# Scattered token rows that carry both routing weights: one row buffer with a weight on each side, sent without rewriting the weight in between

## The chip, the cores and the metric

The kernel runs on one core of a Trainium2 chip. The metric is the device time of one execution in microseconds (us), the median of the runs shown. The engines are named as the profile names them: PE (TensorE matmul; PEld is its weight load), DVE (VectorE), ACT (ScalarE), POOL (GpSimd), SP (SyncE, which here only issues DMAs).

## The reference, cut to what matters

Two layers work on `x` (4 batches of 1024 rows of 256 floats) and a context of 4 x 64 rows. The first layer shifts and compresses a memory, adds it to `x`, normalizes, and then runs a mixture of experts: each of the 4096 rows goes to its top 2 of 8 experts, and the two results are added with weights that are the square roots of a softplus.

```python
logits = jnp.einsum('btd,ed->bte', X, routing_W) + expert_bias
activation = jnp.sqrt(jax.nn.softplus(logits))
top_vals, top_idx = jax.lax.top_k(activation, K)          # K = 2
combine = jnp.sum(jax.nn.one_hot(top_idx, E) * top_vals[..., None], axis=-2)
...
hdn = jax.nn.silu(jnp.einsum('nd,edh->enh', Xf, rW1) + rb1[:, None, :])   # h = 128
y = jnp.einsum('enh,ehd->end', hdn, rW2) + rb2[:, None, :]
routed = jnp.einsum('ne,end->nd', cf, y).reshape(B, T, d)
return shared + routed
```

The second layer is a cross attention with 16 heads and another mixture of 8 experts with hidden width 384. The change touches only the routed experts of the first layer.

## The kernel before, in words

Every engine has its own program, written out by hand in the order in which it runs; semaphores tie them together. A tile is 128 rows, and there are 32 tiles. The first layer's experts are worked in two groups `g` of 16 tiles (`LT = 16`).

**Choosing.** `choose(g)` on DVE finds the two experts of each row and, through `places`, the place of each row in a table in DRAM, `xs_dram` (`XS`). A slot is 128 places of that table, all of one expert; each group has 40 slots (`LS = 40`), so 80 in all. `choose(g)` ends by writing the first weight into column `D` of the row buffer `N0` (line 1679) and the second into `m2` (line 1680), and signals `rout` (line 1682).

**Sending.** A row of `N0` is 260 floats: 256 data, the weight, three zeros. `send_rows(g)` on POOL waits for `rout` and writes each tile of `N0` to `xs_dram` by an indirect DMA, one for the first expert of its rows (`k = 0`) and one for the second (`k = 1`): 32 sends a group, 64 in all, on line 541. Between the two the weight in the row has to be replaced. So POOL sends 16 tiles with the first weight, then for each half of the group waits until those sends have landed (line 554), copies the second weights into the rows (line 555), drains, and sends the eight tiles again:

```python
for t, done in parts:
    po.wait_ge(s[done], 16 * half * (g + 1))
    po.tensor_copy(N0[:, t:t + half, D:D + 1], m2[:, t:t + half].rearrange("p (t a) -> p t a", a=1))
    po.drain()
    send(1, t, t + half, "l_sc2")
```

POOL runs `send_rows(0)`, `send_rows(1)` and then collects group 0's results (line 566).

**The slots.** SP, in `routed_rows(g)`, waits for all of the group's sends, loads slot `j` into one of eight buffers `fx` (line 397; six slots ahead) and stores the result `fy` (line 405). PE transposes the slot (`xpose`, line 857), multiplies by the first weight matrix (`up`), and by the second (`down`). For each slot PE and DVE read the slot's expert number into a register (`value_load`; TENSOR_LOAD in the lists below). DVE copies the expert's weights to `fw1` (line 1700) and the transposed rows to `fxT` (line 1702). ACT does the silu (line 1236) and scales the result by the weight that came with the rows (line 1242). PE runs `routed(0)`, then `shared(1)` (the shared expert of the second half), then `routed(1)`, and after a meeting of all engines comes the second layer. `shared_add` on DVE (line 1688) is put between slots. In the second layer rows go to `xs_dram` too, by line 616, with both weights in the row; its experts' results are scattered by line 628.

Of the kernel before, what the change touches and what calls it, by code (L numbers as in the profile page):

```python
# [36 lines left out]
P = 128  # L37
NB, T, D = 4, 1024, 256
DC = D // P
S = 64  # L40
# [48 lines left out]
def build(nc, x, ctx_in, conv_w, conv_b, rout_w, rout_b, sw1, sb1, sw2, sb2, rw1, rb1, rw2, rb2,  # L89
          wq, bq, wk, bk, wv, bv, wo, bo, wr, w1, w2, w3, out):  # L90
    st = ExitStack()
    with st:
        st.enter_context(nc.allow_non_contiguous_dma(reason="bias columns and router weights, small"))

        def sb(name, shape, dt=F32, stack=st):
            return stack.enter_context(nc.sbuf_tensor(name, shape, dt))
# [57 lines left out]
        wcol = sb("wcol", [P, 4])  # L154
# [17 lines left out]
        N0 = sb("N0", [P, TILES, XW], stack=s1)  # L172
# [26 lines left out]
        fx = [sb(f"fx{k}", [P, XW], stack=s2)[:, :] for k in range(XB)]  # L199
# [29 lines left out]
        def row_tile(m):  # L229
# [46 lines left out]
            l_sa l_sb l_sc2 l_nr l_tp l_xa l_xd l_lg l_lt l_tn l_ev l_su l_hs l_sy l_xu  # L276
            f_tp f_xt f_h f_hs f_y f_ys
            l_ga l_gb
            n_st n_q n_r n_ra wr_p wr_c t_p xt_a ro_p ro_sb
# [40 lines left out]
        def _(sp):  # L320
# [7 lines left out]
            def memory_rows(b):  # L328

                t0, k = b * BT, S // RATE  # L330
                sp.dma_start(N0[:, t0:t0 + 4, 0:D],
                             x[b, k:k + CONV, :].rearrange("(t p) d -> p t d", p=P)).then_inc(s[f"s_in{b}"], 16)
                sp.dma_start(N0[:, t0 + 4:t0 + 7, 0:D],
                             x[b, CONV + S:T - S, :].rearrange("(t p) d -> p t d", p=P)).then_inc(s[f"s_in{b}"], 16)
                sp.dma_start(N0[0:S, t0 + 7, 0:D], x[b, T - S:T, :]).then_inc(s[f"s_in{b}"], 16)
                sp.dma_start(N0[S:P, t0 + 7, 0:D], ctx_in[b]).then_inc(s[f"s_in{b}"], 16)

# [44 lines left out]
            def routed_rows(g):  # L382

                for done in ("l_sa", "l_sb"):
                    sp.wait_ge(s[done], 8 * LT * (g + 1))
                sp.wait_ge(s["l_sc2"], 16 * LT * (g + 1))
# [57 lines left out]
            for sent in ("l_sa", "l_sb"):  # L444
                sp.wait_ge(s[sent], 8 * LT * LG + 16 * FREED)
# [27 lines left out]
        def _(po):  # L473
# [38 lines left out]
            po.memset(N0[:, :, D:XW], 0.0)  # L512
# [25 lines left out]
            def send(k, t0, t1, done):  # L538

                for t in range(t0, t1):  # L540
                    po.indirect_dma_start(  # L541
                        XS, bass.IndirectOffsetOnAxis(ap=slot[k][:, t:t + 1], axis=0),
                        N0[:, t, :], None).then_inc(s[done], 16)

            def send_rows(g):
# [3 lines left out]
                half = LT // 2  # L549
                parts = [(LT * g, "l_sa"), (LT * g + half, "l_sb")]  # L550
                for t, done in parts:
                    send(0, t, t + half, done)
                for t, done in parts:
                    po.wait_ge(s[done], 16 * half * (g + 1))
                    po.tensor_copy(N0[:, t:t + half, D:D + 1], m2[:, t:t + half].rearrange("p (t a) -> p t a", a=1))
                    po.drain()
                    send(1, t, t + half, "l_sc2")
# [1647 lines left out]
```

## Time and profile before

| what | value |
|---|---|
| time, median of 3 runs | 926.6 us (926.23, 926.6, 931.65) |
| the profiled execution: its own time | 930.99 us |
| its span in the profile | 929.2 us |
| granted TensorE clock, mean share of full | 0.933 |
| busy PE / DVE / ACT / POOL | 85% / 55% / 53% / 46% |
| sends of line 541 | 64, together 64.3 us busy |
| PE's share of the chain that ended last | 54% |

The span is what the profile's rows add up to; the execution's own time is 1.8 us longer. The profiled execution was 4.4 us slower than the median of the timed runs. A share of the span is a mean over stages with different limits, so the rows further down are read by stage.

### The profile page before, as it was taken

The numbers are of one execution on the slowest core, as the hardware profiler recorded it, in microseconds if no ns is written. First come the engines' busy times: TensorE is split into PE (matmuls) and PEld (weight loads), VectorE is DVE, ScalarE is ACT, GpSimd is POOL, SyncE is SP. The second block draws the span as 40 slices with busy tenths as digits, with TensorE's granted clock in tenths as the row PEclk, the third lists the DMA queues.
The fourth block names the chain that finished last, engine by engine and source line by source line (L and its number), as shares of the span: only waits on it lengthen the run. The fifth ranks groups of instructions, "written<-read, shape, count | busy, mean of one in ns | idle before, by whom it ended". The sixth has DMA issues, their size and how long they took to land.

```text
span 929.2 us, 16520 instructions
## 1 busy us (share of the span) xinstructions
PE 792.1 (85%) x4538; PEld 684.7 (74%) x4538; DVE 509.5 (55%) x1345; ACT 490.0 (53%) x1374; POOL 429.3 (46%) x398
## 2 busy tenths in 40 slices
PE   2989883579999679999998999785789999999992
PEld 1636542479688568999987888674689999999991
DVE  5847851245265558889888878672122222244242
ACT  1458641146466468888776686341334444444440
POOL 2201657610577258988645678435552222222221
PEclk9899995589999889999998999898789999999996
DMA  8799974456699694384230244613332222256524
GB/s 260 267 298 341 318 254 144 127 163 203 156 201 242 173 333 79 62 203 84 59 115 1 80 149 137 199 47 103 97 98 75 69 67 66 70 180 200 187 89 158
DMA packets 122115, 143.02 MB, mean 154 GB/s; under 512 B 10391, under 2 KB 113612, under 8 KB 121004
## 3 DMA queue, kind: packets, MB, share of 16 engines
q1 hardware_dynamic: 90520, 92.03, 33.2%
q0 software_dynamic: 19856, 38.88, 15.4%
q10 hardware_dynamic: 11654, 11.05, 3.7%
q8 instruction: 44, 0.72, 0.3%
q14 instruction: 41, 0.34, 0.1%
HBM read 71.28 MB, written 70.65 MB: 153 GB/s over the span
## 4 chain that ended last, share of the span: by engine, by line
PE 54%; DVE 15%; ACT 9%; issue 7%; another core or an unknown queue 6%; DVEq 5%; DMA 2%; SPq 1%; POOL 1%; POOLq 0%; ACTq 0%
PE psum L678 29%; PE psum L1042 5%; ACT pr L1324 5%; PE psum L1047 5%; PE psum L1043 5%; DVE nmx L2013 2%; PE psum L1056 2%; DVE sm L2018 2%; PE psum L857 2%; PE psum L954 2%; DVE prl L2028 2%; PE psum L1026 2%; DVEq L2019 1%; DVE wlo L1983 1%
## 5 line engine op out<-in xcount | busy, mean ns | idle before, releaser
L628 POOL DMA_INDIRECT yk_dram<-ys,L x71 | 70.0, 986 | 202.2 <-ACT ys L1396 200.3
L566 POOL DMA_INDIRECT X<-yl_dram,slots_y x64 | 104.1, 1627 | 73.2 <-DMA yl_dram<-fy 50.8
L1042 PE MATMUL psum<-whi,xTh 128*128 x284 | 111.0, 391 | 22.8 <-ACT xTh L1378 22.7
L1324 ACT ACTIVATE pr<-psum,nmx 128x64 f32<-128x64 f32 x512 | 108.1, 362 | 35.2 <-DVE nmx L2013 35.2
L2107 DVE TENSOR_TENSOR hs<-psum,hs 128x384 f32<-128x384 f32 x71 | 39.7, 560 | 153.6 <-PE psum L1047 100.0
L678 PE MATMUL psum<-w_sb,cz 128*128 x426 | 104.7, 382 | 1.5 <-ACT ys L1396 1.2
L541 POOL DMA_INDIRECT xs_dram<-N,slots x64 | 64.3, 1005 | 87.3 <-DVEq L1681 50.6
L1043 PE MATMUL psum<-wlo,xTh 128*128 x284 | 97.8, 344 | 0.0
L608 POOL TENSOR_TENSOR pr<-pr,sm 128x1024 f32<-128x1024 f32 x32 | 63.8, 1992 | 57.5 <-DVE sm L2020 56.9
L678 PEld LDWEIGHTS psum<-w_sb,cz 128*128 128x128 f32 x426 | 75.8, 191 | 10.1 <-issue 2.6
L1047 PE MATMUL psum<-whi,xTl 128*128 x284 | 75.4, 347 | 3.4 <-DVE xTl L2126 3.4
L616 POOL DMA_INDIRECT xs_dram<-N,slots x64 | 66.6, 1040 | 21.3 <-issue 18.0
L1042 PEld LDWEIGHTS psum<-whi,xTh 128*128 128x128 f32 x284 | 55.0, 194 | 27.6 <-issue 26.1
L678 PE MATMUL psum<-rw_sb,fh 128*128 x160 | 57.2, 441 | 19.3 <-issue 10.6
L1384 ACT ACTIVATE cz<-psum 128x384 f32<-128x384 f32 x69 | 33.8, 490 | 71.7 <-PE psum L1056 52.8
L1390 ACT ACTIVATE hs<-psum 128x384 f32<-128x384 f32 x71 | 34.9, 492 | 60.4 <-PE psum L1047 43.5
L678 PE MATMUL psum<-fxT,fw 128*128 128x128 f32 x320 | 53.3, 292 | 9.1 <-issue 8.6
L1236 ACT ACTIVATE fh<-psum,fw 128x128 f32<-128x128 f32 x80 | 29.3, 366 | 52.2 <-remote 32.2
L1396 ACT ACTIVATE ys<-psum,wcol 128x256 f32<-128x256 f32 x71 | 33.6, 474 | 43.6 <-PE psum L678 40.4
L1043 PEld LDWEIGHTS psum<-wlo,xTh 128*128 128x128 f32 x284 | 55.3, 195 | 1.6
L1047 PEld LDWEIGHTS psum<-whi,xTl 128*128 128x128 f32 x284 | 52.8, 194 | 4.4 <-DVE xTl L2126 4.3
L1700 DVE COPY fw<-rw_sb 128x257 f32 x80 | 25.7, 321 | 54.5 <-ACT fh L1236 35.6
(338 smaller groups left out, 1917.1 us busy)
## 6 DMA issues: line engine op xcount, KB each, us to landing
fx<-xs_dram SPq DMA_DIRECT2D x80, 130.0 KB
xs_dram<-fill SPq DMA_DIRECT2D x4, 2600.0 KB
yl_dram<-fy SPq DMA_DIRECT2D x80, 128.0 KB
xs<-xs_dram SPq DMA_DIRECT2D x71, 130.0 KB
wlo<-in_L_ffn_W_dram SPq DMA_DIRECT2D x4, 1536.0 KB, 7.2
ym<-yk_dram ACTq DMA_DIRECT2D x12, 512.0 KB
xs_dram<-cz SPq DMA_DIRECT2D x1, 5200.0 KB, 27.5
xs_dram<-cz SPq DMA_DIRECT2D x8, 650.0 KB
```

What stands on the lines that cost most here:

```text
L541: po.indirect_dma_start(XS, bass.IndirectOffsetOnAxis(ap=slot[k][:, t:t + 1], axis=0), N0[:, t, :], None).then_inc(s[done], 16)
L566: po.indirect_dma_start(X[:, t, :], None, YL[b // 2], bass.IndirectOffsetOnAxis(ap=slot_y[k][:, t:t + 1], axis=0), compute_op=ALU.add).the ...
L608: po.tensor_tensor(v, v, sm[n % 2][:, :].rearrange("p (a b) -> p a b", b=1).to_broadcast([P, NHEAD, S]), ALU.mult).then_inc(s["a_pn"], 1)
L616: po.indirect_dma_start(XS1, bass.IndirectOffsetOnAxis(ap=slot[k][:, t:t + 1], axis=0), row_tile(t)[:, part], None).then_inc(s[done], 16)
L628: po.indirect_dma_start(YK, bass.IndirectOffsetOnAxis(ap=yid[:, j:j + 1], axis=0), ys[j % YB], None).then_inc(s[f"y_out{j % YB}"], 16)
L678: return nc.tensor.matmul(o, l, r, start=start, stop=stop)
L1042: nc.tensor.matmul(o, xTh[b][:, c, :], wh[c], start=c == 0, stop=False)
L1043: nc.tensor.matmul(o, xTh[b][:, c, :], wl[c], start=False, stop=False)
L1047: last = nc.tensor.matmul(o, xTl[b][:, c, :], wh[c], start=False, stop=c == DC - 1)
L1324: last = act(pr[b][:, S * h:S * h + S], bank[2 * b + h // 8][:, S * (h % 8):S * (h % 8) + S], ACT.Exp, bias=nmx[:, h:h + 1])
L1390: act(hs[j % 2], bank[2 + j % 2][:, 0:H1], ACT.Silu).then_inc(s["e_hs"], 1)
L2107: tt(hs[j % 2], bank[4 + j % 2][:, 0:H1], hs[j % 2], ALU.mult).then_inc(s["e_hg"], 1)
```

## The change

The row buffer gets a weight on each side: two columns, the data, two columns (`X0 = 2`). `choose` writes the first weight into column `X0 - 1`, left of the data, and the second into column `X0 + D`, right of it. The send for the first expert takes columns 0 to 257 (left weight and data), the one for the second takes columns 2 to 259 (data and right weight); each writes 258 floats at an element address, so that the data always fall on columns 2 to 257 of the place in `xs_dram`. The table was zeroed, so one of a place's two weight columns holds the weight and the other zero. Neither rewriting nor waiting is left between the sends. The weight of a place is the sum of both columns: the eight `fx` buffers become one tile `fx8`, and DVE adds both columns for four slots at once into `wcol`, after its copies for slot `j` with `j % 4 == 1`, once the loads of the next two slots have landed. ACT scales by `wcol`, and in every fourth slot first waits for DVE's copy of two slots later.

```diff
-        wcol = sb("wcol", [P, 4])
+        wcol = sb("wcol", [P, XB])
...
-        N0 = sb("N0", [P, TILES, XW], stack=s1)
+        N0w = sb("N0", [P, TILES, XW], stack=s1)
+        N0 = N0w[:, :, X0:X0 + D]
...
-        fx = [sb(f"fx{k}", [P, XW], stack=s2)[:, :] for k in range(XB)]
+        fx8 = sb("fx8", [P, XB, XW], stack=s2)
+        fx = [fx8[:, k, :] for k in range(XB)]
...
-                for done in ("l_sa", "l_sb"):
-                    sp.wait_ge(s[done], 8 * LT * (g + 1))
-                sp.wait_ge(s["l_sc2"], 16 * LT * (g + 1))
+                for k in range(2):
+                    sp.wait_ge(s[f"l_s{k}{g}"], 16 * LT)
...
             def send(k, t0, t1, done):
 
+                part = (slice(0, X0 + D), slice(X0, XW))[k]
                 for t in range(t0, t1):
                     po.indirect_dma_start(
-                        XS, bass.IndirectOffsetOnAxis(ap=slot[k][:, t:t + 1], axis=0),
-                        N0[:, t, :], None).then_inc(s[done], 16)
+                        XS1, bass.IndirectOffsetOnAxis(ap=slot[k][:, t:t + 1], axis=0),
+                        N0w[:, t, part], None).then_inc(s[done], 16)
...
                 po.wait_ge(s["rout"], g + 1)
-                half = LT // 2
-                parts = [(LT * g, "l_sa"), (LT * g + half, "l_sb")]
-                for t, done in parts:
-                    send(0, t, t + half, done)
-                for t, done in parts:
-                    po.wait_ge(s[done], 16 * half * (g + 1))
-                    po.tensor_copy(N0[:, t:t + half, D:D + 1], m2[:, t:t + half].rearrange("p (t a) -> p t a", a=1))
-                    po.drain()
-                    send(1, t, t + half, "l_sc2")
+                for k in range(2):
+                    send(k, LT * g, LT * g + LT, f"l_s{k}{g}")
...
-                    act(fy[j % YB], bank[(7, 5)[j % 2]][:, 0:D], ACT.Copy, scale=fx[j % XB][:, D:D + 1]).then_inc(s["f_ys"], 1)
+                    if j % 4 == 0:
+                        ac.wait_ge(s["f_xt"], j + 3)
+                    act(fy[j % YB], bank[(7, 5)[j % 2]][:, 0:D], ACT.Copy, scale=wcol[:, j % XB:j % XB + 1]).then_inc(s["f_ys"], 1)
...
-                ts(slots[:, :, t0:t0 + n], hot2[:, :, 0:n], float(base), None, ALU.add)
+                for k in range(2):
+                    ts(slots[:, k, t0:t0 + n], hot2[:, k, 0:n], float(XW), float(XW * base + X0 * k), ALU.mult, ALU.add)
...
-                tt(N0[:, t0:t0 + n, D], sp_x[:, 0, :], sp_r[:, 0, :], ALU.mult)
-                tt(m2[:, t0:t0 + n], sp_x[:, 1, :], sp_r[:, 1, :], ALU.mult)
+                tt(N0w[:, t0:t0 + n, X0 - 1], sp_x[:, 0, :], sp_r[:, 0, :], ALU.mult)
+                tt(N0w[:, t0:t0 + n, X0 + D], sp_x[:, 1, :], sp_r[:, 1, :], ALU.mult)
...
+                    if j % 4 == 1:
+                        k = j % XB - 1
+                        for i in (1, 2):
+                            ve.wait_ge(s[f"xs_in{(j + i) % XB}"], 16 * ((j + i) // XB + 1))
+                        if j > XB:
+                            ve.wait_ge(s["f_ys"], j - 5)
+                        tt(wcol[:, k:k + 4], fx8[:, k:k + 4, X0 - 1], fx8[:, k:k + 4, X0 + D], ALU.add)
+                        ve.drain()
```

In POOL's program, this stood in a row for group 0 and into group 1. L541 is the send, L555 the copy of the second weights; what a row waits for is in brackets.

```order
L541 DMA xs_dram<-N,slots 10240x260 [waits rout,zeroed0]
L541 DMA xs_dram<-N,slots 10240x260 x15
L555 COPY N<-m 128x8 [waits l_sa]
L541 DMA xs_dram<-N,slots 10240x260 x8
L555 COPY N<-m 128x8 [waits l_sb]
L541 DMA xs_dram<-N,slots 10240x260 x8
L541 DMA xs_dram<-N,slots 10240x260 [waits rout,zeroed1]
```

Now the same place reads, through both groups and on to the first collecting DMA (L562 of the changed kernel, L566 of the one before):

```order
L544 DMA xs_dram<-N,slots 2662400x1 [waits rout,zeroed0]
L544 DMA xs_dram<-N,slots 2662400x1 x31
L544 DMA xs_dram<-N,slots 2662400x1 [waits rout,zeroed1]
L544 DMA xs_dram<-N,slots 2662400x1 x31
L562 DMA X<-yl_dram,slots_y 128x256 [waits ys_out2,ys_out1,ys_out3,ys_out0,l_xu]
```

The copies and their waits are gone, and each group is 32 sends in a row.

In DVE's program, the first slots of group 0 (slots 0, 1 and the start of 2) stood like this:

```order
L1700 COPY fw10<-rw1_sb 128x257
L1702 COPY fxT0<-psum 128x256 [waits f_tp]
L1697 TENSOR_LOAD eid
L1697 ISA x2
L1700 ISA
L1700 COPY fw11<-rw1_sb 128x257
L1702 COPY fxT1<-psum 128x256 [waits f_tp]
L1697 TENSOR_LOAD eid
```

Now there is an addition behind slot 1's copy, which waits for the loads of slots 2 and 3 (line numbers of the changed kernel, one less than before):

```order
L1699 COPY fw10<-rw1_sb 128x257
L1701 COPY fxT0<-psum 128x256 [waits f_tp]
L1696 TENSOR_LOAD eid
L1696 ISA x2
L1699 ISA
L1699 COPY fw11<-rw1_sb 128x257
L1701 COPY fxT1<-psum 128x256 [waits f_tp]
L1708 TENSOR_TENSOR wcol<-fx8 128x4 [waits xs_in3,xs_in2]
L1696 TENSOR_LOAD eid
```

The same addition stands behind every fourth slot after it, 20 times in all, ahead of the register load and the copies of the slot that follows.

## Rows read from the trace of the kernel before

**Rows 1.** The chain that ended last, its longest wait: start us, us, what.

```profile
144.48 13.61 another core or an unknown queue
```

**Rows 2.** Busy time by stage: window, length, busy us (instructions), PEclk, DMA share, GB/s.

```profile
145.00:170.00 25.00, 7.53 (x26) 5.85 (x26) 2.25 (x6) 0.73 (x2) 17.06 (x19) 0.50 0.41 134
...
193.00:236.00 43.00, 42.99 (x280) 39.97 (x280) 24.66 (x65) 26.31 (x64) 0.00 (x0) 0.94 0.62 180
...
252.00:312.00 60.00, 55.98 (x353) 48.10 (x354) 34.80 (x88) 35.31 (x84) 42.38 (x27) 1.00 0.93 211
```

**Rows 3.** Timeline of POOL, sends and copies: start, us, instruction, idle before it.

```profile
110.91 0.21 POOL L555 COPY N<-m 128x8 f32<-128x8 f32 x1
118.11 1.17 POOL L541 DMA_INDIRECT xs_dram<-N,slots  x1 [6.99 <-issue]
...
134.71 0.98 POOL L541 DMA_INDIRECT xs_dram<-N,slots  x1 [6.37 <-issue]
...
144.84 0.96 POOL L541 DMA_INDIRECT xs_dram<-N,slots  x1 [0.30 <-issue]
...
163.84 0.96 POOL L541 DMA_INDIRECT xs_dram<-N,slots  x1 [0.30 <-issue]
...
168.07 0.98 POOL L541 DMA_INDIRECT xs_dram<-N,slots  x1 [3.06 <-issue]
...
180.80 0.98 POOL L541 DMA_INDIRECT xs_dram<-N,slots  x1 [2.33 <-issue]
...
189.68 0.96 POOL L541 DMA_INDIRECT xs_dram<-N,slots  x1 [0.30 <-issue]
```

**Rows 4.** Timeline of the other engines around the first slots.

```profile
142.44 0.16 DVE L1680 TENSOR_TENSOR m<-sp_x,sp_r 128x16 f32<-128x16 f32 x1
143.97 0.29 DVE L1700 COPY fw<-rw_sb 128x257 f32 x1 [1.07 <-issue]
146.11 5.66 SPq L397 DMA_DIRECT2D fx<-xs_dram  x7
149.00 1.09 PE L857 MATMUL psum<-ident,fx 128*128 128x128 f32 x4 [7.82 <-DMA fx<-xs_dram]
151.20 0.63 PE L857 MATMUL psum<-ident,fx 128*128 128x128 f32 x2
158.11 0.37 ACT L1236 ACTIVATE fh<-psum,fw 128x128 f32<-128x128 f32 x1 [13.63 <-remote]
164.41 0.42 DVE L1702 COPY fxT<-psum 128x256 f32<-128x256 f32 x1 [5.50 <-remote]
170.56 0.32 SPq L405 DMA_DIRECT2D yl_dram<-fy  x1
187.76 0.32 SPq L405 DMA_DIRECT2D yl_dram<-fy  x1
192.29 0.37 ACT L1236 ACTIVATE fh<-psum,fw 128x128 f32<-128x128 f32 x1 [4.55 <-remote]
```

**Rows 5.** Timeline of the second layer: a run of sends and the engine behind it.

```profile
630.83 0.97 POOL L616 DMA_INDIRECT xs_dram<-N,slots  x1 [3.30 <-DVEq L1858]
647.41 0.97 POOL L616 DMA_INDIRECT xs_dram<-N,slots  x1 [0.30 <-issue]
648.73 0.56 DVE L2107 TENSOR_TENSOR hs<-psum,hs 128x384 f32<-128x384 f32 x1 [13.51 <-remote]
```

**Rows 6.** Timeline of slots at full pace; the last two rows in group 1.

```profile
207.40 0.44 SPq L397 DMA_DIRECT2D fx<-xs_dram  x1
209.30 0.42 DVE L1702 COPY fxT<-psum 128x256 f32<-128x256 f32 x1
211.61 0.61 PE L678 MATMUL psum<-fxT,fw 128*128 128x128 f32 x4
...
273.80 0.44 SPq L397 DMA_DIRECT2D fx<-xs_dram  x1
278.36 0.20 PEld L857 LDWEIGHTS psum<-ident,fx 128*128 128x128 f32 x2 [0.25 <-DMA fx<-xs_dram]
```

More of the change, by code:

```diff
@@ L275, in build @@
             b2_in b2_hi b2_lo b2_zero sw_in rw_in
-            l_sa l_sb l_sc2 l_nr l_tp l_xa l_xd l_lg l_lt l_tn l_ev l_su l_hs l_sy l_xu
+            l_s00 l_s10 l_s01 l_s11 l_nr l_tp l_xa l_xd l_lg l_lt l_tn l_ev l_su l_hs l_sy l_xu
             f_tp f_xt f_h f_hs f_y f_ys
             l_ga l_gb
-            n_st n_q n_r n_ra wr_p wr_c t_p xt_a ro_p ro_sb
+            n_st n_q n_r wr_p wr_c t_p xt_a ro_p ro_sb
             spa spd r_m r_pt rout sc1 sc2
@@ L330, in memory_rows @@
                 t0, k = b * BT, S // RATE
-                sp.dma_start(N0[:, t0:t0 + 4, 0:D],
+                sp.dma_start(N0[:, t0:t0 + 4, :],
                              x[b, k:k + CONV, :].rearrange("(t p) d -> p t d", p=P)).then_inc(s[f"s_in{b}"], 16)
-                sp.dma_start(N0[:, t0 + 4:t0 + 7, 0:D],
+                sp.dma_start(N0[:, t0 + 4:t0 + 7, :],
                              x[b, CONV + S:T - S, :].rearrange("(t p) d -> p t d", p=P)).then_inc(s[f"s_in{b}"], 16)
-                sp.dma_start(N0[0:S, t0 + 7, 0:D], x[b, T - S:T, :]).then_inc(s[f"s_in{b}"], 16)
-                sp.dma_start(N0[S:P, t0 + 7, 0:D], ctx_in[b]).then_inc(s[f"s_in{b}"], 16)
+                sp.dma_start(N0[0:S, t0 + 7, :], x[b, T - S:T, :]).then_inc(s[f"s_in{b}"], 16)
+                sp.dma_start(N0[S:P, t0 + 7, :], ctx_in[b]).then_inc(s[f"s_in{b}"], 16)
             def x_rows(b):
@@ L442, in _ @@
             weights(2)
-            for sent in ("l_sa", "l_sb"):
-                sp.wait_ge(s[sent], 8 * LT * LG + 16 * FREED)
+            for sent in ("l_s01", "l_s11"):
+                sp.wait_ge(s[sent], 16 * LT + 16 * FREED)
             weights(3)
@@ L511, in _ @@
                 po.memset(vbd[k], 0.0)
-            po.memset(N0[:, :, D:XW], 0.0)
+            po.memset(N0w[:, :, 0:X0], 0.0)
+            po.memset(N0w[:, :, X0 + D:XW], 0.0)
             po.memset(upper[:, :], 0.0)
@@ L614, in scatter @@
                 for t in range(t0, t1):
-                    done = ("l_sa", "l_sb")[k] if t < FREED else f"sc{k + 1}"
+                    done = ("l_s01", "l_s11")[k] if t < FREED else f"sc{k + 1}"
                     po.indirect_dma_start(
@@ L856, in xpose @@
                     for c in range(DC):
-                        last = nc.tensor.transpose(bank[j % 2][:, c * P:c * P + P], fx[j % XB][:, c * P:c * P + P], ident[:, :])
+                        last = nc.tensor.transpose(bank[j % 2][:, c * P:c * P + P], fx[j % XB][:, X0 + c * P:X0 + c * P + P], ident[:, :])
                     last.then_inc(s["f_tp"], 1)
@@ L1579, in memory_add @@
                         t, n = b * BT + i, {3: k, 7: S}.get(i, P)
-                        stt(X[0:n, t, :], N0[0:n, t, 0:D], rstd[0:n, t:t + 1], X[0:n, t, :], ALU.mult, ALU.add)
+                        stt(X[0:n, t, :], N0[0:n, t, :], rstd[0:n, t:t + 1], X[0:n, t, :], ALU.mult, ALU.add)
                     t = b * BT + BT - 1
-                    tt(X[S:P, t, :], X[S:P, t, :], N0[S:P, t, 0:D], ALU.add)
+                    tt(X[S:P, t, :], X[S:P, t, :], N0[S:P, t, :], ALU.add)
                 ve.drain()
@@ L1595, in rows_in @@
                     for t in range(QT * q, QT * q + QT):
-                        last = ts(N0[:, t, 0:D], X[:, t, :], mean[:, t:t + 1], rstd[:, t:t + 1], ALU.subtract, ALU.mult)
+                        last = ts(N0[:, t, :], X[:, t, :], mean[:, t:t + 1], rstd[:, t:t + 1], ALU.subtract, ALU.mult)
                     last.then_inc(s["l_nr"], 1)
```

## The prediction

> **What bounds the kernel now.** I first asked the chain that ended last for the stages in which it does not run through work. Its longest piece is a wait of 13.61 us at 144.48, for something that the profile cannot name [rows 1], so I read busy time by stage there. From 145 to 170 us PE is busy 7.53 of 25 us, DVE 2.25, ACT 0.73, while POOL is busy 17.06; the clock stands at its lower level, 0.50 of full, that is 1.2 GHz, on a PE that is mostly idle. From 193 to 236 PE is busy 42.99 of 43 us [rows 2]. This is one and the same work, the 40 slots of `routed(0)`. So the stage has a slow part in which nobody computes much, and a fast part that PE bounds.
>
> Then I laid POOL's timeline beside the others'. POOL sends group 1 from 144.84 to 189.68 + 0.96 = 190.64 us [rows 3]. PE starts on the slots at 149.00, when the first load lands. Then ACT waits 13.63 us for its first silu and DVE 5.50 us for a copy, both for something remote; PE had turned the rows for that copy (slot 2, begun at 151.20) by 151.83, 12.6 us before. Six slots are stored until the sends end (the first at 170.56, the last at 187.76), and ACT's last long wait ends at 192.29, 1.65 us after POOL's last send; from there all goes at full pace [rows 4]. The 34 slots left take 236.0 - 192.3 = 43.7 us, 1.28 each (a slot stored in the 43 us of rows 2: 1.27). The second layer shows the same thing by itself: a run of sends from 630.83, its last at 647.41 and done 0.97 later, and DVE, which had waited 13.51 us for something remote, goes on 0.35 us after it [rows 5]. I read this as: **while POOL issues these sends back to back, signals between the other engines get through slowly, and a pause or the end of the run lets them through.** The profile shows the coincidence in both layers, not the path. What counts then is when POOL's last send of group 1 is out, and how many slots got through before.
>
> The times below are those of the profiled execution (930.99 us, span 929.2 and 1.8 around it), which was 4.4 us above the median of 926.6. I apply the difference to the median.
>
> **The pauses that go.** Each copy of second weights is followed by a pause: 0.21 + 6.99 us from 110.91 to 118.11, 6.37 before 134.71, 3.06 before 168.07, 2.33 before 180.80, 18.75 us together and 0.83 more for the four copies [rows 3]. The pauses of group 0 are worth little: without them its 32 sends, begun at 88.8, are out by about 131, but group 1's may not start before `rout`, which DVE gives after its row at 142.44, at 142.60 [rows 4]. They started at 144.84, so they now start at about 142.9: 1.9 us gained, and 11 of the 13.8 us of these two pauses go into waiting for `rout`. Group 1's 32 sends take 31 x 1.267 + 0.96 = 40.2 us (15 steps from 144.84 to 163.84 are 19.00 us). A send of 258 floats at an element address is that of the second layer, 0.97 in a run, no dearer [rows 5]. So **the last send is out at 183.1 instead of 190.64: -7.5 us.**
>
> The other end of the stage moves as well. Group 0's sends land earlier than the loads of 146.11 now need them, so PE has its rows when it is done with the shared expert; DVE's first weight copy (143.97 + 0.29) then decides, and the first slot can go through DVE at 144.3, where before PE's first transposes came at 149.00 [rows 4]. That alone gains nothing if the run of sends holds the slots back anyway.
>
> **How many slots get through.** Before, six, with two pauses to help. Now there is none. If the run had 40.2 us as before's 41.6 us (149.0 to 190.64, six slots, 0.14 per us), it would be 6; at the pace of the unbroken piece from 149 to 165, about one slot in 16 us, it is 2.5; the new run also begins together with the slots, and in the second layer the trouble began some 4 us after the run's start (648.73 - 13.51 = 635.2 against 630.83) [rows 5], which is room for one or two slots more. I take 4, nearest to the unbroken piece, with bounds of 1 and 7. Two slots fewer are done by then: +2 x 1.28 = +2.6. From the resumption on, 1.65 us after 183.1, there are then 43.7 + 2.6 us: the stage ends at 231.0 instead of 236.0, **-5.0 us** (7 slots: -8.8; 1 slot: -1.1). What follows, `shared(1)` and `routed(1)`, is behind it on PE, and POOL's collecting waits for the stores, so the gain is handed on.
>
> **What DVE's addition costs.** 20 additions of 128 x 4; the nearest row is 0.16 us for 128 x 16 [rows 4]. 3.2 us on an engine that is busy 24.66 of 43 us [rows 2]: alone it is hidden by DVE's waiting for ACT. The price is the new wait behind slot `j`'s copy, for the load of slot `j + 2`. Queued behind it on DVE are the register load and both copies of slot `j + 1`, for which PE's `up(j + 1)` waits; then ACT, through its new wait. In group 0 at full pace that load is issued at 207.40, DVE's copy ends at 209.72, and PE wants the next one at 211.61 [rows 6]. Take off 0.16 + 0.30 + 0.42 for the work, about 0.55 for the register load and 0.03 for the rest (it took up to 1.07 before 143.97 [rows 4]): the load may land at 210.15, 2.75 us after its issue, without harm. No row gives a landing at full pace. Nearest, and also a 130 KB load of that queue: 146.11 to 149.00 us, 2.89 [rows 4]. Farthest, in group 1 with the DMA engines 0.93 busy instead of 0.62: issued at 273.80, waited for until 278.36, 4.56 us [rows 2, 6]. There the slots are slower, 60 us for 40, 1.5 each, so four of them leave 0.9 more: 3.65. A late addition also gives the next its time, so about half of the lateness is paid. With 2.89 and a slower register load 0.2 us is paid at each of 8 additions of group 0, none in group 1: **+1.6**. Nothing is the lower end; with 4.56 throughout it is 8 x 0.9 + 10 x 0.45 = 11.7.
>
> The Trainium skill, DMA: Bandwidth & Descriptors, in the table of two cost components, gives a DMA about 2.0 us fixed and its bytes at 436 GB/s, an estimate of 2.3 us for such a load; by it the wait would cost nothing and the sum would be -5.0. The trace's 2.89 and 4.56 are above it, and I go by them.
>
> Everything else is nothing: DVE writes the second weight into the row instead of `m2` at the same 0.16, ACT reads its scale from another column, and the data start 8 bytes further, as they already do in the second layer.
>
> **The sum:** -5.0 + 1.6 = -3.4 us: 927.6 for an execution like the profiled one, **923.2 us** against the median, some 0.4%.
>
> **Rivals.**
> - **The slots run ahead of the sends.** PE, ACT and DVE begin at 144.3, when POOL has only just begun. If the trouble takes a longer run to build up, or the signals that were held up were an effect of starting in the middle of one, many more slots get through: with 12, -7.5 - 6 x 1.28 + 1.6 = -13.6, 913.0. If sends did not hold up slots at all, the 40 slots would be done near 144.3 + 40 x 1.28 = 195.5, 40 us early. For it: the last of the six stores, at 187.76, came 7 us into a run [rows 3, 4]. Against: ACT's first silu of all waited 13.63 us.
> - **Starved.** An unbroken run lets almost nothing through, 1 slot: -1.1 + 1.6 = +0.5, 927.1. For it: in the second layer nothing moved on DVE for 13.51 us.
> - **DVE waits for loads, and the kernel gets slower.** If loads land as at 278.36, DVE becomes the bound of both stages at every fourth slot: -5.0 + 11.7 = +6.7, 933.3. It decides from a landing of 3.8 us on (8 x 0.5 x 1.05 + 10 x 0.5 x 0.15 = 5.0). Against it: the wait at 278.36 is PE's only one for a load in the 40 slots of group 1.
> - **The change does not give POOL its time back.** The pause may be the queue's need rather than the copy's: with up to 32 sends under way POOL would be held by the queue, and the last send stays at 190: 0 + 1.6, 928.2. Against: the sends in the pieces of 16 ran at an even 1.27 us.
>
> **How the numbers follow.** Chances: the forecast with its bounds (1 to 7 slots without the extreme, small waits) 0.45; slots ahead 0.17; starved 0.15; waits for loads 0.13; no time back 0.10. The range for 8 in 10 goes from 912.0, which takes in 12 slots but not a stage without trouble, to 934.0, which takes in the load rival. About 1% (9.3 us) is what a measurement of this kernel can tell from no change: faster by more than that needs 917.3 or less, the first rival and a little of the forecast's lower end, 0.2; slower by more needs 935.9 or more, only the far end of the load rival and chance in the second layer's stalls, 0.06; the rest, 0.74, is within.
>
> **What the profile after would show.** Right: two runs of 32 sends with no pause, the second from 142.9 to 183; long remote waits of ACT and DVE until about 185; 3 to 6 stores before; the stage's end near 231; additions without waits for fx over 0.5 us. Wrong: if the second run has pauses (no time back); if the slots run at 1.28 us beside the sends (ahead); if waits for fx show on DVE at every fourth slot and the slots of the fast part take more than 1.3 us (loads). The forecast would be most wrong if my reading of sends and signals is a coincidence.

## The result and the profile after

The changed kernel took **969.0 us** (median of 4, 966.7 to 971.8) beside 927.2 us of the kernel before (926.2 to 931.7): ratio 1.042, 95% interval 1.038 to 1.046. It is slower by 4.2%, and outside the predicted range. The profiled execution took 968.01 us, its span was 965.9.

Busy time by stage in the kernel after, with the columns of [rows 2]:

```profile
111.00:118.00 7.00, 0.00 (x0) 0.00 (x0) 2.49 (x10) 0.72 (x2) 5.17 (x7) 0.50 1.00 314
118.00:128.00 10.00, 0.00 (x0) 0.00 (x0) 0.96 (x3) 0.60 (x1) 7.68 (x8) 0.50 0.41 144
...
145.00:170.00 25.00, 20.56 (x101) 12.11 (x98) 14.79 (x51) 10.53 (x18) 0.00 (x0) 1.00 0.23 83
172.00:193.00 21.00, 8.91 (x44) 7.51 (x42) 4.94 (x14) 3.31 (x8) 15.57 (x17) 0.72 0.36 121
193.00:213.00 20.00, 3.08 (x9) 2.21 (x9) 0.79 (x3) 0.84 (x2) 15.43 (x16) 0.50 0.34 119
213.00:236.00 23.00, 17.50 (x104) 15.76 (x105) 10.58 (x29) 10.60 (x25) 0.15 (x1) 0.80 0.46 140
236.00:260.00 24.00, 23.46 (x157) 21.19 (x156) 13.63 (x41) 14.53 (x35) 0.00 (x0) 1.00 0.62 178
```

The slow stage of [rows 2] has moved from 145 to 172, and there is a new one from 111 to 128, in which PE does nothing at all. Both are stretches in which POOL sends. Its timeline after, for [rows 3]; each send between the first two rows and between the third and fourth has an idle 0.30 or 0.31 us before it, so there is no pause:

```profile
88.77 1.06 POOL L544 DMA_INDIRECT xs_dram<-N,slots  x1 [50.85 <-DVEq L1680]
...
129.40 0.97 POOL L544 DMA_INDIRECT xs_dram<-N,slots  x1 [0.30 <-issue]
172.55 0.97 POOL L544 DMA_INDIRECT xs_dram<-N,slots  x1 [42.18 <-DVEq L1680]
...
212.18 0.97 POOL L544 DMA_INDIRECT xs_dram<-N,slots  x1 [0.30 <-issue]
273.91 1.67 POOL L562 DMA_INDIRECT X<-yl_dram,slots_y  x1 [60.76 <-DMA yl_dram<-fy]
```

Group 1's first send waited 42.18 us for `rout`; it stood at 144.84 before [rows 3]. What kept `rout` is in the timeline of the other engines, the counterpart of [rows 4]:

```profile
106.86 1.13 PE L674 MATMUL psum<-wo_sb,kvbd 128*128 128x256 f32 x4 [1.73 <-ACT st_r L1165]
...
110.53 0.60 ACT L1165 ACTIVATE st_r<-psum 128x512 f32<-128x512 f32 x1 [3.71 <-remote]
113.39 0.60 ACT L1165 ACTIVATE st_r<-psum 128x512 f32<-128x512 f32 x1 [2.26 <-remote]
123.21 0.60 ACT L1165 ACTIVATE st_r<-psum 128x512 f32<-128x512 f32 x1 [9.23 <-remote]
133.05 0.60 ACT L1165 ACTIVATE st_r<-psum 128x512 f32<-128x512 f32 x1 [9.24 <-remote]
...
133.70 8.78 PE L674 MATMUL psum<-xT,sw_sb 128*128 128x512 f32 x16 [25.70 <-ACT st_r L1165]
...
171.58 0.18 DVE L1679 TENSOR_TENSOR N<-sp_x,sp_r 128x16 f32<-128x16 f32 x1
...
177.58 0.32 SPq L406 DMA_DIRECT2D yl_dram<-fy  x1
198.17 0.42 DVE L1701 COPY fxT<-psum 128x256 f32<-128x256 f32 x1 [8.34 <-remote]
207.97 0.37 ACT L1232 ACTIVATE fh<-psum,fw 128x128 f32<-128x128 f32 x1 [12.83 <-remote]
216.20 0.32 SPq L406 DMA_DIRECT2D yl_dram<-fy  x1
```

PE's last group of `fold` (the folding of the weights that comes ahead of the shared expert) starts at 106.86 and is 1.13 us long. ACT empties what PE has left in PSUM at 110.53, 113.39, 123.21 and 133.05, each time after a wait for something remote, and PE stands for 25.70 us waiting for ACT. That is the sign by which the prediction knew the hold-up in `routed(0)`, now in group 0's run of sends as well. DVE's last weights of group 1, ahead of `rout`, were at 142.44 before [rows 4]; now they are at 171.58, 29 us later. PE from 111 to 135 us, in the kernel before and then in the one after:

```profile
111.00:135.00 24.00, 19.72 (x97) 10.62 (x95) 13.52 (x40) 10.01 (x17) 8.51 (x11) 1.00 0.91 297
111.00:135.00 24.00, 1.30 (x2) 0.79 (x3) 3.44 (x12) 3.24 (x6) 14.80 (x16) 0.50 0.53 174
```

Where the 37 us lie, by three marks of POOL's timeline: the first collecting transfer comes at 273.91 instead of 241.44 (+32.5), the attention's first product (`pr`) at 372.99 instead of 334.91 (+5.6 more), and the end 36.7 later (1.4 less again). Before these, group 1's first send is 27.7 late. So there is **a large loss ahead of group 1's routing and a small one between the collecting and the attention**, where `routed(1)` runs.

### The profile page after: what moved, and what is told of

Same layout as the page of the kernel before. It is cut to its first block, busy times and chain, and to the rows that moved or that the text cites. A ratio compares the mean times of both kernels' runs of the same rounds, so it can differ in the third digit from the quotient of the medians.

```text
span 965.9 us, 16576 instructions
## 1 busy us (share of the span) xinstructions
PE 792.1 (82%) x4538; PEld 682.1 (71%) x4538; DVE 509.9 (53%) x1367; ACT 492.2 (51%) x1374; POOL 425.8 (44%) x395
## 4 chain that ended last, share of the span: by engine, by line
PE 49%; DVE 15%; ACT 8%; issue 8%; another core or an unknown queue 8%; DVEq 5%; DMA 4%; SPq 1%; POOL 1%; ACTq 0%; POOLq 0%
PE psum L674 25%; ACT pr L1322 5%; PE psum L1038 5%; PE psum L1043 5%; PE psum L1039 5%; DVE nmx L2020 3%; PE psum L1052 2%; DVE sm L2025 2%; PE psum L950 2%; DMA fx<-xs_dram 2%; PE psum L1022 1%; DVEq L2026 1%; PE psum L853 1%; DMA X<-in_x_dram 1%
## 5 line engine op out<-in xcount | busy, mean ns | idle before, releaser
L562 POOL DMA_INDIRECT X<-yl_dram,slots_y x64 | 104.0, 1625 | 83.1 <-DMA yl_dram<-fy 60.8
L1240 ACT ACTIVATE fy<-psum,wcol 128x256 f32<-128x256 f32 x80 | 38.0, 476 | 53.0 <-PE psum L674 29.0
L674 PEld LDWEIGHTS psum<-fxT,fw 128*128 128x128 f32 x320 | 44.1, 200 | 27.1 <-DVE fxT L1701 15.4
L1394 ACT ACTIVATE ys<-psum,wcol 128x256 f32<-128x256 f32 x71 | 33.8, 476 | 44.5 <-PE psum L674 40.6
```

The costliest lines, as they stand in the source:

```text
L562: po.indirect_dma_start(X[:, t, :], None, YL[b // 2], bass.IndirectOffsetOnAxis(ap=slot_y[k][:, t:t + 1], axis=0), compute_op=ALU.add).the ...
L674: return nc.tensor.matmul(o, l, r, start=start, stop=stop)
L1240: act(fy[j % YB], bank[(7, 5)[j % 2]][:, 0:D], ACT.Copy, scale=wcol[:, j % XB:j % XB + 1]).then_inc(s["f_ys"], 1)
```

## The experiments

Three theories. **A**: an unbroken run of sends holds up signals between the other engines, and the removed pauses in group 0 had been letting them through. **B**: the new form of send (258 floats at an element address) holds up more than the old one. **C**: the waits of DVE's addition for four slots are the small loss. The groups of runs after the first comparison fell on five chips, and which one turned out to matter more than any edit:

| kernels run together | the kernel before there | chip |
|---|---|---|
| the first comparison | 927.2 us | not on record |
| e1 to e4 | 875.4 | 10 |
| e5 to e8 | 928.3 | 1 |
| e9 to e12 | 873.8 | 8 |
| e13 to e16 | 873.2 | 11 |
| e17 and e18 | 925.1 | 9 |

The kernel before takes either 925 to 928 us or 873 to 875. Ratios are always to the kernel before in the same group of runs. Each chip was used in one group only, so "on this chip" below also means "in this group of runs": whether the chip itself or something else of that group makes the difference was not tested.

### Chip 10: pauses back, old form, more pauses

**e1, pauses at their old places:**

```
-                for k in range(2):
-                    send(k, LT * g, LT * g + LT, f"l_s{k}{g}")
+                send(0, LT * g, LT * g + LT, f"l_s0{g}")
+                for h in range(2):
+                    po.drain()
+                    send(1, LT * g + LT // 2 * h, LT * g + LT // 2 * h + LT // 2, f"l_s1{g}")
```

> The changed kernel with a drain of POOL put back at the three places of each group where a pause stood before: 16 sends, drain, 8, drain, 8; nothing is rewritten. Theory A (the unbroken run of 32 sends holds up the other engines' signals, and pauses let them through): the shared expert's part before rout ends near 143 us again instead of 172, the 30 us of group 0 come back and part of group 1's; 928 to 938 us. Rival B (the new form of the sends, 258 floats at an element address, holds up the others more than rows of 260 did): the trace from 98 us on still shows remote waits, over 950 us. Rival C (DVE's addition and its waits): what stays above 927 with the pauses back is its cost, 3 to 10 us.

**e2, the old form of send without pauses** (each row carries both weights, so the results are scaled by their sum; the places in `slots` are row numbers again, which is not shown):

```
-                        XS1, bass.IndirectOffsetOnAxis(ap=slot[k][:, t:t + 1], axis=0),
-                        N0w[:, t, part], None).then_inc(s[done], 16)
+                        XS, bass.IndirectOffsetOnAxis(ap=slot[k][:, t:t + 1], axis=0),
+                        N0w[:, t, :], None).then_inc(s[done], 16)
```

> The changed kernel with the old form of the sends (whole rows of 260 floats at a row address) and still no pauses; both weights then stand in each row, so the first layer's expert results are scaled by the sum of both weights (wrong values). Theory A (length of the run): as slow as the changed kernel, 955 to 975 us. Rival B (form of the sends): 925 to 940 us.

**e3, a pause after every fourth send** (`if t % 4 == 3: po.drain()` in `send`):

> The changed kernel with a drain of POOL behind every fourth send of both groups. Theory A: no long remote waits in either group; group 0 costs nothing, in group 1 the slots run nearly at their pace beside the sends, 890 to 925 us, below both kernels. Rival B (form): 940 to 970, since the same 64 sends are made. If the pause itself costs more than the run: about 930 to 940.

**e4, at most two sends under way** (in `send`; the sends of a group take its two semaphores in turn, and each waits until the one before the last has landed):

```
+                    i = k * LT + t - t0
+                    done = f"l_s{i % 2}{t // LT}"
+                    if i >= 2:
+                        po.wait_ge(s[done], 16 * (i // 2))
```

> The changed kernel without drains, but POOL waits before each send until the send before the last has landed, so that two are under way at most. Theory A in the form that what counts is how many sends are queued and not yet landed: remote waits vanish, 890 to 920 us. Theory A in the form that only an idle, drained POOL lets signals through: no better than the changed kernel where landings are fast (group 1), 940 to 970 us. In group 0, where the DMA engines are full, sends may get slow enough to delay rout's user: up to 10 us more.

Measured: e1 886.7 us (ratio 1.0145, interval 1.006 to 1.023), e2 877.8 (1.0046, 1.001 to 1.009), e3 899.6 (1.030, 1.021 to 1.039), e4 894.7 (1.023, 1.015 to 1.031), beside 875.4 of the kernel before. None of the theories had foreseen a kernel before of 875 us. There is no hold-up in sight here: during the last 32 sends of the second layer (613 to 666 us in e1) PE is busy all 53 us, and the same in the other three. So the pauses only cost: e1 takes 9 us more than e2, e3 22 and e4 17 more (e2 has the old form of send as well, so these are not the pauses alone). In e3 and e4 PE is busy only 7.1 and 9.9 of 25 us from 145 to 170: the slots of group 0 wait for its last rows, which slower sends deliver later (SP issues the first loads of `fx` at 160.69 in e3 and 156.96 in e4, at 146.07 in e1). This group tells A and B apart nowhere; it tells that the hold-up is not there on every chip. e3 and e4 were meant to tell what lets the signals through, the pause or the number of sends under way, and neither was run where there is a hold-up.

### Chip 1: the hold-up is there

**e5, the changed kernel again:**

> The changed kernel, unaltered, beside the kernel before on the chip of this group of runs. Two cases, told apart by the time of the kernel before. Where it is near 927 us (the signals between the engines are held up by unbroken sends, as in the first comparison): all theories expect about 969 us, ratio 1.04, group 1's first send near 172 us. Where it is near 875 us (as in the first four experiments): theory A (only the unbroken run of sends costs) expects the change to cost nothing there, 873 to 880 us, and the groups of TensorE in the stretch 111 to 145 us near those of the row form; theory B (short rows at float addresses are held up more than whole rows) expects more than the row form's 878 by over 5 us; theory C (VectorE's addition waits for loads) expects what the addition's waits sum to, about 2 us, in both forms alike.

**e6, pauses in group 0 alone** (e1's edit under `if not g`):

> The changed kernel with the pauses put back in group 0's sends alone (16, pause, 8, pause, 8); group 1's 32 sends stay unbroken. On a chip where the kernel before takes about 927 us: theory A expects the 30 us ahead of group 1's routing back, 969 - 30 = about 939 us, with group 1's first send near 143 us; theory B expects about 965. On a chip where it takes about 875 us: the pauses can only cost there; if they cost by delaying group 0's rows to the slots, about 5 us more than the changed kernel without them, and if only group 1's pauses cost, nothing.

**e7, e1's kernel again:**

> The changed kernel with the pauses back in both groups, on the same chip as the unaltered one. On a chip where the kernel before takes about 927 us: theory A expects about 932 (927 and 3 to 5 us for the addition's waits for loads), theory B over 945, theory C 932 as well but with the addition's waits of 5 us in the rows. On a chip where it takes about 875 us: about 9 us more than the changed kernel, as the pauses cost in the first group of runs (886.7 against the row form's 877.8).

**e8, e2's kernel again:**

> The changed kernel with whole rows of 260 floats sent at row addresses, as the kernel before sends them, and no pause; each row carries both weights, so the results are scaled by their sum. On a chip where the kernel before takes about 927 us: theory A expects about 969 as for the changed kernel, since the run of sends is as unbroken; theory B expects about 930. On a chip where it takes about 875 us: theory A expects the time of the changed kernel within 3 us, theory B at least 5 us less than the changed kernel.

Measured, beside 928.3 us of the kernel before:

| kernel | us | ratio (interval) | group 1's first send after group 0's | first collecting transfer after group 0's first send |
|---|---|---|---|---|
| e5, as changed | 964.4 | 1.042 (1.031 to 1.052) | 82.0 us | 178.1 us |
| e6, pauses in group 0 | 947.2 | 1.022 (1.012 to 1.032) | 66.3 | 165.2 |
| e7, pauses in both | 942.1 | 1.017 (1.007 to 1.027) | 64.9 | 150.5 |
| e8, old form of send | 958.7 | 1.035 (1.026 to 1.044) | 77.6 | 176.8 |
| before (the first comparison) | 927.2 | | 56.1 | 152.7 |

The loss comes back as 4.2%. Pauses in group 0 alone give 17 us back, group 1's 5 more: 22 of 36. In the timelines of POOL of e5, e6 and e7, group 1's first send:

```profile
172.23 0.97 POOL L544 DMA_INDIRECT xs_dram<-N,slots  x1 [40.41 <-DVEq L1680]
```

```profile
154.02 0.97 POOL L544 DMA_INDIRECT xs_dram<-N,slots  x1 [11.31 <-DVEq L1686]
```

```profile
158.47 0.96 POOL L544 DMA_INDIRECT xs_dram<-N,slots  x1 [9.80 <-DVEq L1682]
```

(e7's group 0 began at 93.55, e6's at 87.74, e5's at 90.25 and e8's at 93.78; the table takes that out. e8's marks are those of its slowest execution, 969.32 us, 10.6 above its median.) And PE in the stretch 111 to 135 us, where the run of e5 is unbroken and e6 pauses, windows of e5, then e6:

```profile
111.00:135.00 24.00, 2.90 (x4) 1.34 (x5) 3.90 (x15) 3.28 (x5) 15.95 (x17) 0.50 0.67 217
```

```profile
111.00:135.00 24.00, 21.45 (x76) 9.27 (x76) 8.33 (x22) 10.98 (x18) 9.66 (x10) 0.90 0.90 294
```

PE is busy 2.9 of 24 us without pauses, 21.5 with them. That the missing pauses are the main cause is shown; that what they let through is signals, as A says, is the reading of the remote waits. A had expected about 939 of e6 and about 932 of e7, though; 8 and 10 us more stayed. With the pauses at their old places group 1's first send still comes 9 to 10 us later than in the one trace of the kernel before with a hold-up (65 to 66 us after group 0's first, against 56), but in e7 the first collecting transfer is as early as there (150.5 against 152.7). B had expected about 930 of e8, and its 958.7 refutes it as the main cause; 5.6 us less than e5, with intervals that overlap, leave it room for a small part, and so does PE in e8's unbroken run, busy 11.3 of 24 us in the same stretch.

### Chip 8: no hold-up, and the small loss by itself

**e9, the kernel before, for its profile:**

> The kernel before itself, for its profile on the chip of this group of runs: ratio 1.00. What is read from it is the time from the first collecting transfer to the start of the attention. It took 93.5 us in the kernel before on the first chip and 100.6 to 101.8 us in every variant of the changed kernel with VectorE's addition for four slots, on both chips tried since. Theory C (those 7 us are the addition's waits for loads) expects 93 to 95 us here as well; the theory that they are the chip's expects 100 to 101.

**e10, one addition per slot, ahead of the slot's own copy** (in DVE's `routed`; ScalarE's wait for a later slot goes as well):

```
+                    k = j % XB
+                    if j >= XB:
+                        ve.wait_ge(s["f_ys"], j - XB + 1)
+                    tt(wcol[:, k:k + 1], fx8[:, k:k + 1, X0 - 1], fx8[:, k:k + 1, X0 + D], ALU.add)
                     nc.vector.tensor_copy(fxT[j % 2].rearrange("p c n -> p (c n)"), bank[j % 2][:, 0:D]).then_inc(s["f_xt"], 1)
-                    if j % 4 == 1:
...
-                        tt(wcol[:, k:k + 4], fx8[:, k:k + 4, X0 - 1], fx8[:, k:k + 4, X0 + D], ALU.add)
-                        ve.drain()
```

> The changed kernel, but VectorE adds one slot's two weights just ahead of that slot's copy of the turned rows (40 additions instead of 10, none waiting for a later slot's load), and ScalarE doesn't wait for a later slot. Theory C expects 5 to 8 us less than the changed kernel: about 957 on a chip where the kernel before takes about 927, about 870 where it takes about 875, and about 94 us from the first collecting transfer to the attention. If the waits of the four-slot addition cost nothing, the 30 added instructions of 0.1 us cost up to 3 us.

(The expectation's counts are one group's: there are 80 additions instead of 20 in the whole layer.)

**e11, e10 and e1 together:**

> The one addition per slot, and the pauses back in both groups of sends. If the hold-up by unbroken sends (A) and the waits of the addition (C) are all of the loss, this equals the kernel before within 1%, whatever the chip: about 930 us where the kernel before takes about 927; about 878 where it takes about 875. If something of the new layout costs besides, it stays 1% to 1.7% above.

**e12, no addition at all** (ScalarE takes the left weight alone, so rows that came on the right are scaled wrongly):

> The changed kernel without any addition: ScalarE scales every slot by the row's first weight column alone, so rows that came on the right get the wrong weight. Shows what the addition can cost at most. Theory C expects the time of the kernel with one addition per slot within 2 us, and 5 to 8 us less than the changed kernel; the theory that the addition is free expects the changed kernel's time.

Measured, beside 873.8: e9 874.1 (ratio 1.000, 0.998 to 1.002), e10 867.8 (0.992, 0.989 to 0.995), e11 872.6 (0.999, 0.996 to 1.002), e12 867.9 (0.992, 0.988 to 0.996). From the first collecting transfer to the attention it is 93.7 us in the kernel before (e9), 95.9 in e10, 95.0 in e11, 93.9 in e12. Every kernel so far with the addition for four slots had 99 to 102 there (99.1 in the first trace after, 99.6 in e3, 100.6 to 101.8 in the others), on chips with and without the hold-up. One addition per slot costs what none costs. So these 5 to 8 us are the change's and not the chip's: C holds.

### Chip 11: no hold-up either, with the unaltered changed kernel

**e13, the changed kernel; e14, e11's kernel; e15, e10's kernel:**

> The changed kernel, unaltered. Where the kernel before takes about 928 us: 964 to 969, as twice before. Where it takes about 875: 7 us of the addition's waits above the kernel with one addition per slot (ratio 0.992), so ratio 0.998 to 1.003.

> One addition per slot and the pauses in both groups of sends. Where the kernel before takes about 928 us: if hold-up and addition are the whole loss, 928 to 935 (942 of the pauses alone, less the 7 that the addition's waits took on the other chips); if the new form of the sends costs more besides, 938 to 942. Where it takes about 875: ratio 0.999 again.

> One addition per slot, no pauses. Where the kernel before takes about 928 us: the hold-up stays, so 955 to 960 (964 less 5 to 8). Where it takes about 875: ratio 0.992 again.

**e16, e10 with a pause after every 8 sends:**

```
+                for h in range(4):
+                    if h:
+                        po.drain()
+                    send(h // 2, LT * g + LT // 2 * (h % 2), LT * g + LT // 2 * (h % 2) + LT // 2, f"l_s{h // 2}{g}")
```

> One addition per slot and a pause after every 8 sends of each group, three per group instead of two. Where the kernel before takes about 928 us: if the signals need only a few pauses, faster than with two pauses by up to 5 us, since none of the runs is longer than 11 us; if a pause's own 6 to 8 us counts more, 3 to 8 us slower. Where it takes about 875: 6 to 8 us slower than the kernel with two pauses in group 0, since each pause of group 0 puts its last row off.

Measured, beside 873.2: e13 878.0 (ratio 1.008, 1.005 to 1.011), e14 874.2 (0.999, 0.996 to 1.002), e15 867.0 (0.995, 0.993 to 0.997), e16 875.9 (1.003, 1.000 to 1.006). The changed kernel is 0.8% slower where nothing is held up, a little more than expected. Beside e15 it takes 10.9 us more, which is the whole price of the addition for four slots and its waits here; 5 to 8 had been expected. e16's third pause costs 1.7 us beside e14, where 6 to 8 had been expected. In e13's windows one sees that the same unbroken run does nothing to PE here:

```profile
111.00:135.00 24.00, 20.14 (x102) 11.87 (x102) 14.03 (x43) 11.79 (x20) 13.66 (x15) 1.00 1.02 322
145.00:170.00 25.00, 23.09 (x148) 20.13 (x146) 14.46 (x39) 13.47 (x32) 19.25 (x19) 0.98 0.83 257
603.00:655.00 52.00, 52.00 (x304) 49.41 (x303) 14.53 (x42) 25.02 (x66) 39.52 (x42) 1.00 0.42 133
```

The last row is the stretch of the second layer's last 32 sends, which no edit touched: PE is busy all 52 us. In the first trace after, the same 32 sends take from 666 to 734:

```profile
666.00:734.00 68.00, 47.48 (x238) 43.77 (x237) 11.57 (x35) 19.65 (x53) 39.98 (x42) 0.85 0.30 99
```

The two marks around `routed(1)`, in POOL's timeline of e13, then of e15:

```profile
207.35 1.67 POOL L562 DMA_INDIRECT X<-yl_dram,slots_y  x1 [24.46 <-DMA yl_dram<-fy]
...
309.32 1.90 POOL L604 TENSOR_TENSOR pr<-pr,sm 128x1024 f32<-128x1024 f32 x1 [6.79 <-DVE sm L2027]
```

```profile
206.35 1.67 POOL L562 DMA_INDIRECT X<-yl_dram,slots_y  x1 [22.17 <-DMA yl_dram<-fy]
...
299.91 1.90 POOL L604 TENSOR_TENSOR pr<-pr,sm 128x1024 f32<-128x1024 f32 x1 [6.57 <-DVE sm L2021]
```

102.0 us against 93.6, and 93.7 in e9. Between the marks of e13, waits of DVE's addition and of ACT (us in total, times, longest):

```profile
ACT fy L1240 <- DVE fxT L1701: 10.7, 7, 2.7
...
DVE wcol L1708 <- DMA fx<-xs_dram: 7.7, 5, 2.5
...
PE psum L674 <- DVE fxT L1701: 6.0, 7, 1.8
```

and one of the additions with what follows it, timeline of e13:

```profile
271.36 0.17 DVE L1708 TENSOR_TENSOR wcol<-fx 128x4 f32<-128x4 f32 x1 [2.47 <-DMA fx<-xs_dram]
272.77 0.42 DVE L1701 COPY fxT<-psum 128x256 f32<-128x256 f32 x1
...
273.25 0.71 PE L674 MATMUL psum<-fxT,fw 128*128 128x128 f32 x4 [1.49 <-DVE fxT L1701]
273.31 0.47 ACT L1240 ACTIVATE fy<-psum,wcol 128x256 f32<-128x256 f32 x1 [2.69 <-DVE fxT L1701]
```

The addition of four slots waits 2.47 us for the load of a slot that nobody else wants yet. The next copy is late behind it, PE waits for that copy, and ACT for the same copy by the change's new wait. How long the loads of `fx` issued from 256 to 275 us in e13 take:

```profile
DMA to landing us min/median/max: 4.2/4.8/5.3
```

The Trainium skill, DMA: Bandwidth & Descriptors, in the table of two cost components for a DMA that GpSimd issues, gives about 2.0 us fixed and the bytes at 436 GB/s. The prediction's estimate from it was 2.3 us for such a load, which SP issues here; this stretch shows twice that, and the measurement decides.

### Chip 9: the hold-up is there, with both cures

**e17, e11's kernel, and e18, e10's kernel:**

> One addition per slot and the pauses in both groups. Where the kernel before takes about 928 us: 928 to 935 if hold-up and addition are the whole loss, 938 to 942 if the form of the sends costs more besides. Where it takes about 875: ratio 0.999, as twice.

> One addition per slot, no pauses. Where the kernel before takes about 928 us: 955 to 960, ratio about 1.03. Where it takes about 875: ratio 0.992 to 0.995, as twice.

Measured, beside 925.1: e17 931.8 (ratio 1.010, 1.005 to 1.016), e18 954.9 (1.033, 1.027 to 1.040). e17 takes 94.2 us between the two marks, e7 took 101.0: C again, here on a chip with the hold-up. The first collecting transfer of e17 is at 242.19. The pauses are worth 23 us to this kernel on this chip, and cost it 5 (e11, chip 8) and 7 us (e14, chip 11) without the hold-up. The four versions, as ratios to the kernel before:

| kernel | with the hold-up | without it |
|---|---|---|
| as changed | 1.042 (the first comparison), 1.042 (e5) | 1.008 (e13) |
| with the pauses | 1.017 (e7) | 1.0145 (e1) |
| with one addition per slot | 1.033 (e18) | 0.992 (e10), 0.995 (e15) |
| with both | 1.010 (e17) | 0.999 (e11), 0.999 (e14) |

## Why the prediction was wrong

- **The step that failed** is "the pauses of group 0 are worth little". It took `rout` of group 1 as fixed at 142.60, let the unbroken run of group 0 end at 131 without asking whom it holds up, and so had group 1's first send 1.9 us earlier, at 142.9. It came at 172.55, 27.7 us later than before. (By its own figures 11.9 of the two pauses' 13.8 us go into waiting, not 11; nothing hangs on that.) The prediction had named the mechanism itself and then applied it to one of the two runs only. Group 0's second 16 sends go beside `fold` and the shared expert, through which `rout` comes. The weights that `rout` waits for came 29 us later (171.58 against 142.44), and putting the pauses back there alone gave 17 of 36 us back (e6), the pauses in both groups 22 (e7).
- **Why it looked safe.** Under the first 16 sends PE was busy 22.0 of 23 us in the trace before, so a run beside this stage seemed harmless. In fact those 16 ended in a pause. The trace before shows no run of 32 beside it; the nearest rows were group 1's run and the second layer's, and both showed the trouble. No rival was this one: the slower side had the addition's waits and, by half a microsecond, the starved slots of `routed(0)`.
- **The last send.** A run of 32 was to take 40.2 us; it took 40.6 (172.55 to 213.15). Right. That it would end 7.5 us earlier fell with its start.
- **Slots that get through.** 4 forecast, 3 stored before the run's end (stores at 177.58, 181.65, 195.16). Right in kind. But from the last send to the first collecting transfer it took 60.8 us instead of 50.8. Before, six slots were stored by then, so three fewer explain 3 x 1.28 = 3.8 of these 10. PE had only 17.50 of 23 us busy after the run, at a granted clock of 0.80. How the rest divides between recovery, clock and the addition was not taken apart.
- **The addition.** Sized at +1.6 with ends 0 and 11.7. The mechanism (DVE late for the next copy) is what the rows show, and the term was mis-sized: 10.9 us in all on a chip without hold-up (e13 against e15), close to its far end of 11.7. 8.4 of them lie between the marks (102.0 against 93.6), where it had nothing; in the first comparison it was 5.6 there. The landing time was taken from a stage with little traffic, 2.89 us, for group 1 too, where the DMA engines are 0.93 busy; there the one row of 4.56 us that the prediction held to be far is near the median (4.8 in the stretch shown, 4.2 over all of e13's loads between the marks). ACT's new wait may add to it. e10 removes both waits together, so their shares stay open.
- **The reading of sends and signals** that the forecast would be "most wrong" without has held as far as the runs go: on two chips the pauses alone gave 22 and 23 us. The path is not shown, nor what it is about a run that does it (sends without a gap, how many are under way, or their traffic): the runs that would tell, e3 and e4, fell on a chip without the hold-up. That it is there on some chips only was foreseen by no part.
- **The gain.** Where nothing is held up, the removed pauses bring the first collecting transfer 2.8 us nearer to group 0's first send (e13 against e9), and with one addition per slot the kernel is 0.5% to 0.8% faster than before (e15, e10). The change as made loses it again, mostly in `routed(1)`.
- **What stays open.** With both cures there is 1.0% left on chip 9 (6.7 us), and none on chips 8 and 11. So something of the change seems to cost with the hold-up alone, as far as one group of runs can say. The form of the sends could be it (e8's 5.6 us), or that a drain without the wait for landings pauses less well than the old copy; neither was tried together with the cures on such a chip. The place is open too, since the kernel before was traced with a hold-up only in the first comparison. Beside that trace e17's group 1 starts 9.9 us later after group 0's first send (65.9 against 56.1), but its first collecting transfer comes as early (153.0 against 152.7).

No version beats both kernels everywhere. e10's is faster than both without the hold-up, and 3.3% slower than the kernel before with it.

## What to carry to other kernels

A pause in a queue of transfers may be useful to engines that never wait on it: before taking it out, list what runs beside each of the runs that grow longer, not only beside the one on the path. An operation that serves several loop steps at once waits for the youngest of them; price that wait with landing times of the busiest stage it runs in. And where one kernel takes 6% longer on one chip than on another, measure an edit on both: its sign may differ (one addition per slot without pauses: 0.5% to 0.8% faster, 3.3% slower).

## What the runs showed of the hardware

- **While POOL issues runs of scattering sends, the other engines are held up on some chips and not on others.** With the same step of 1.27 us from send to send, PE is busy 47.5 of 68 us during the second layer's last 32 sends in the first trace after, and 52.0 of 52 in e13. The kernel before takes 925 to 928 us in three groups of runs, 873 to 875 in three; chip and group are not told apart. Between its two traces (span 929.2, and 867.9 in e9) 31.3 of the 61.3 us lie before the attention. Another 27 arise during the second layer's last 32 sends and the scatters just behind them (the first scatter of line 628 is 33.8 us later, at 608.04 against 574.28, the 22nd 61.0 later, at 722.58 against 661.57).
- **How soon it sets in differs from stage to stage.** In group 0, sixteen sends before a pause left PE between 15.3 and 22.0 of 23 us busy (88 to 111 us, e6 and the kernel before), while sends 17 to 32 without one left it between 1.30 (after) and 11.3 (e8) of 24 us (111 to 135). In group 1 of the kernel before, PE was busy 7.53 of the first 25 us of the run [rows 2].
- **A drain after 16 sends lasts 5.7 to 8.4 us in group 0** (6.99 before, 5.65 in e17, 8.44 in e11) **and 3.1 to 6.5 in group 1** (3.06 before, 6.52 in e9), though each send occupies POOL for 0.97. It lasts as long where nothing is held up, and there buys nothing.
- **A 130 KB load took 4.2 to 5.3 us to land** (median 4.8) from 256 to 275 us in e13, with the DMA engines 0.93 busy, and 2.2 to 4.9 (median 2.9) from 150 to 200 us of the same execution, with them 0.79 busy.
